# The first deformable tile of each group placed 24 plan units behind its places

## The reference, cut to what matters

```
x = x + L0(gn(x))   # focal modulation, three depthwise convolutions
x = x + L1(gn(x))   # fp8-quantised gated MLP per pixel
x = x + L2(gn(x))   # 7x7 circular convolutions, gates, scan over 8 steps
x = x + L3(gn(x))   # deformable 3x3 convolution
# L3: offsets = conv3x3(x) -> per pixel and tap a place (py, px)
#     val = sum of the 4 corners' values * bilinear weights  (9 taps, 64 channels)
#     out = einsum(val, kernel) + bias
```

## Time and profile before

| | us |
|---|---|
| median of 3 runs (lowest to highest) | 5486.43 (5479.14 to 5493.68) |
| the profiled execution's own time | 5502.65 |
| its span, first to last instruction | 5500.9 |
| busy: PE, DVE, POOL, ACT | 3035.7, 3300.6, 2874.9, 1728.7 |

### The profile page before, as it was taken

The page is one execution under the profiler, slowest core; times in us unless marked ns, Lnnn a source line. Parts: engine busy times, 40 slices in busy tenths (PEclk is TensorE's granted clock), DMA queues, the critical chain, the costliest instruction groups (busy, mean ns, idle before and its releaser), DMA issues. The chain is left out here.

```text
span 5500.9 us, 92960 instructions
## 1 busy us (share of the span) xinstructions
PE 3035.7 (55%) x39574; PEld 2637.7 (48%) x39574; DVE 3300.6 (60%) x4063; ACT 1728.7 (31%) x3209; POOL 2874.9 (52%) x2614
## 2 busy tenths in 40 slices
PE   2973235559744466569744466579744463454333
PEld 2872135459633365459633365469633353443222
DVE  4347843575678755565688656574788655454333
ACT  1223424621234235421233235421234242232000
POOL 1000000475566765565566655674666666677776
PEclk9965555569667766659767666659766666655555
DMA  6841184569633585559633576559633564754333
GB/s 164 171 91 22 33 133 138 141 147 224 146 96 102 129 193 169 148 135 222 146 94 105 133 178 173 153 144 236 139 107 98 144 172 136 173 171 131 112 106 93
DMA packets 776703, 763.09 MB, mean 139 GB/s; under 512 B 575185, under 2 KB 652401, under 8 KB 771857
## 3 DMA queue, kind: packets, MB, share of 16 engines
q1 hardware_dynamic: 651873, 417.24, 34.2%
q0 software_dynamic: 124416, 339.90, 21.8%
HBM read 637.12 MB, written 136.73 MB: 141 GB/s over the span
## 5 line engine op out<-in xcount | busy, mean ns | idle before, releaser
L2124 POOL DMA_INDIRECT e_gb<-corner_table,e_idx x2592 | 2860.3, 1104 | 2606.5 <-DMA e_cws<-cw_all 1097.6
L2186 DVE TENSOR_TENSOR e_vw<-e_gb,e_pc 128x1024 f32<-128x1024 f32 x576 | 774.9, 1373 | 710.4 <-DMA e_gb<-corner_table,e_idx 681.0
L2152 PE MATMUL e_pv<-shifts,e_vw 128*128 128x128 f32 x2744 | 536.7, 364 | 480.7 <-DVE e_vw L2193 480.7
L2152 PEld LDWEIGHTS e_pv<-shifts,e_vw 128*128 128x128 f32 x2744 | 440.0, 190 | 513.5 <-DVE e_vw L2193 491.2
L488 PE MATMUL e_pw<-wk,e_vt 128*64 128x64 f32 (+1 forms) x2880 | 324.4, 285 | 351.6 <-DVE e_xr L2204 220.3
L488 PEld LDWEIGHTS e_pw<-wk,e_vt 128*64 128x64 f32 (+1 forms) x2880 | 279.2, 192 | 413.7 <-issue 246.5
L2162 ACT ACTIVATE e_vt<-e_pv 128x512 f32<-128x512 f32 x288 | 183.6, 638 | 731.2 <-PE e_pw L2152 730.4
L502 PE MATMUL b_p<-b_x,b_tt 100*100 100x96 f32 x4096 | 396.2, 258 | 25.7 <-DMA b_tt<-zl_copies 25.0
L502 PEld LDWEIGHTS b_p<-b_x,b_tt 100*100 100x100 f32 x4096 | 388.6, 176 | 29.1 <-DMA b_tt<-zl_copies 28.2
L1921 ACT ACTIVATE f_xall<-f_p 64x384 f32<-64x384 f32 (+2 forms) x320 | 301.7, 1056 | 130.7 <-PE f_p L1816 128.4
L2193 DVE TENSOR_TENSOR e_vw<-e_vw 128x1152 f32<-128x1152 f32 x233 | 331.6, 1423 | 8.0
(11 more groups left out here) (309 smaller groups left out, 7147.3 us busy)
## 6 DMA issues: line engine op xcount, KB each, us to landing
b_tt<-zl_copies SPq DMA_DIRECT2D x256, 234.0 KB, 9.7
b_tt<-zl_copies SPq DMA_DIRECT2D x128, 390.0 KB
e_gb<-corner_table,e_idx POOLq DMA_INDIRECT x2592
d_px<-x_halo SPq DMA_DIRECT2D x32, 1152.0 KB
corner_table<-f_xn SPq DMA_DIRECT2D x128, 288.0 KB
f_xall<-xpad SPq DMA_DIRECT2D x10, 2400.0 KB, 16.7
x_halo<-d_xo SPq DMA_DIRECT2D x128, 144.0 KB
d_wd<-wd_rows SPq DMA_DIRECT2D x8, 1890.0 KB, 30.8
```

Source lines behind the costliest of these rows:

```text
L2124: nc.gpsimd.indirect_dma_start(self.gb[k][:, 4 * q:4 * q + 4, :].rearrange("p a c -> p (a c)"), None, T.table[m], off)\
L2152: last = nc.tensor.matmul(dst, vw[:, a, 2 * q:2 * q + nq, :].rearrange("p k c -> p (k c)"), T.ident[:, :], start=(a == 0), stop=(a == n - ...
L2186: v.tensor_tensor(dst, self.gb[k][:, 4 * k0:4 * k1, :].rearrange("p (k a) c -> p k a c", a=4), bc(w, [128, k1 - k0, 4, C], 3), ALU.mult).t ...
```

## The change

In `plan()`, where all loaded tiles are placed and an image's places have just been written, the next tile's due time is set 24 units later. Everything else follows from it.

```diff
             if StageF.placed(P, k) is not None:
                 if tiles == J * loaded:
-                    due = clock
+                    due = clock + 24.0
                 ready += 1
```

## The result

The kernel after takes 5447.58 us in the median (5443.26 to 5449.61, four runs), the kernel before 5490.06 us beside it (5479.14 to 5499.29, four runs): a ratio of 0.9924 with a 95% interval of [0.9911, 0.9937], 42 us faster. The forecast was 85 us faster. The direction was right and the time lies inside the range, but only half of the gain came.

What follows compares the result with a forecast made beforehand. Stages were taken to set the pace before 4592 us, with VectorE stalled at group starts, and GpSimd's gathers after. Terms -60 - 20 - 5 + 0 = -85 us took the 5486.43 median to 5401 us; 8-in-10 range 5371 to 5460.

Steps and rivals of the forecast that it cites:

- Part 1: Start of the first three groups: moving early tiles behind later steps ends VectorE's stall for gathers, 60.0 us less.
- Part 2: Rest of stage F, behind k11 to k17: VectorE's waits for gathers go, 20 us less, bounds 0 to 52.2.
- Part 3: Last group: GpSimd's wait for D k4's image shortens, 5 us less; bounds -19 and +23.
- Part 4: Phase: every other tile shifts against the stage steps, taken as 0 us, bounds -4 and +34.
- waiting pairs: Nine more stage steps with two tiles behind them, each waiting 3.81 us: the +34 us bound.
- Gathers beside VectorE's work: Start of groups: gathers may slow while VectorE writes, 2.1 us lost per group, making the sum 6 us smaller.
- Only the stall goes, and the phase gives some of it back: Rival, 0.17: groups' starting stall goes, -60 us, but nine more tile pairs wait, +34, giving 5460 us.
- The lead is absorbed: Rival, 0.08: something else paces stage F and the next stage starts no sooner, 5486 us, no change.
- The last group starts late: Rival, 0.09: GpSimd idles at the last group's head, +23 and +12 us, giving 5521 us.

Runs made afterwards that it cites:

- e6_48_rest: e5_48 with tiles 0 and 1 of the first three groups back behind k8 and k9, as in the kernel before: 5451.6 us, ratio 0.9928.
- e1_two_only: Kernel before with only tiles 0 and 1 of the first three groups moved, from behind k8 and k9 to behind k10: 5488.15 us, ratio 0.9988.
- f4_48_kept: Kernel before with tiles due 48 units later in the first three groups, nothing caught up, and 24 in the last: 5416.68 us, ratio 0.9862.
- e4_last_only: Kernel before with only the last group's tiles due 24 units later: 5486.44 us, ratio 0.9987.
- e5_48: Kernel before with tiles due 48 units later in the first three groups, caught up over each group's last tiles, 24 in the last: 5395.32 us, ratio 0.9825.
- e8_back_in_time: The change with its 24 units caught up over the last sixteen tiles of each of the first three groups: 5460.62 us, ratio 0.994.
- e3_both: Kernel before with the first three groups' tiles due 24 units later, caught up by the 16th tile, last group unchanged: 5455.81 us, ratio 0.9929.
- f3_last_48: Kernel before with only the last group's tiles due 48 units later: 5523.48 us, ratio 1.0056.

## Why the prediction was half right

**Part 1, 60 us forecast.** The size is right. Counted from ScalarE's instruction of the round before to the one that follows the norm (line 1985), the round of the first tiles took 66.9, 72.5 and 74.2 us in the kernel before and 51.0, 51.4 and 50.7 us in the one after: 15.9, 21.1 and 23.6 us, together 60.6 (forecast 18.0, 18.3, 23.7). That was luck as far as the reason goes: the reckoning took the times at which tiles end, and these are set by the gathers. The reason given with it, that an idle engine in the middle of a stage costs its full length, was wrong here, where GpSimd was the bound; e6_48_rest shows it right where GpSimd has to wait in turn. e1_two_only removes that wait and its first F stays at 117.1 us. Its norm started here, 4.5 us ahead of before's, with tile 2 weighed in front of it:

```profile
1062.96 0.28 DVE L445 TENSOR_REDUCE gn_ms<-f_p 96x64 f32<-96x128 f32 x1
```

The other 12 us of the 16 come from tile 2's leaving the round, 9 x 1.32 = 11.9 us of gathers.

**Part 2, 20 us forecast, 0 measured. This is the first step that failed**: "The waits go, but what is late next is ScalarE." They don't go (50.5 us for 52.2), and F as a whole gained 60.2 us (20.9, 26.2 and 13.1), no more than Part 1 alone. Behind the first round that is 5.0 and 5.1 us gained in the first two groups and 10.5 lost again in the third. Behind k8, GpSimd is the bound. Gathers issued from the first one to the last places, in the kernel before 81, 82 and 82, in the one after:

```profile
L2124 POOL DMA_INDIRECT e_gb<-corner_table,e_idx x63: 942/949/1972, 1023.2 to 1106.5; - x63
```

and 64 and 72 in the second and third group. That is 18, 18 and 10 fewer, or 23.8, 23.8 and 13.2 us at 1.32 each, 61 in all: the whole gain, and near each group's. It is one effect, and the prediction booked it twice: the tile that leaves the first round (in Part 1) is the tile fewer "up to the same step" (in Part 2). The prediction had the clue in its own sentence, that the five further tiles came "about as close as GpSimd supplies them". Twelve us times the tiles listed was the sum to make; instead the waits of the consumer were added up.

**Part 3, 5 us forecast, 6 to 8 measured.** 7.8 us between the two kernels; over the table the last column is 891.8 to 897.6 us in the four lists with the last group as before (mean 894.9) and 886.9 to 893.9 in the eight that shift it by 24 (mean 889.2, f4_48_kept left out), 5.7 us. Tile 216 was not late, and the load comes earlier as forecast: 12.3 us after D k0's norm (4589.41 - 4577.1) instead of 20.1 (4680.52 - 4660.4), 7.8 us sooner. The gap in front of D k4 shrank by more than that, from 19.12 to 4.09 us. What the prediction did not have is the 13.15 us ahead of tile 222, where gathers land late beside stage D's reads; they use up most of it. In all GpSimd idles 10.9 + 13.15 = 24 us there, where it was 32.3. The first gather to the end was to be 886 us or so; it is 882 (4546.7 to 5427.8, and 0.95 for the last).

**Part 4, 0 forecast, 15 to 28 lost. This is the second step that failed**, a term put at nothing, and with Part 2 it is where the other half went. The lead at the end of F, 60.2 us over three groups, is neither the 45.0 us that arrive at the last group, nor the 32.0 (by line 2052, 4570.02 - 4538.02) against e4_last_only, whose rest was shorter. The bounds (-4 to +34) held it, the price of waiting pairs was its only source and I took the end that was next to nothing. That the shift as such is the cause is excluded by e5_48 and f4_48_kept: with twice the shift their rest is 3206.4 and 3188.9 us. That it is the position ahead of the next k8 finds no support in e8_back_in_time, nor in e3_both. It goes with the tiles taken out of F, but not in proportion: the four lists that take out none have a rest of 3196.6 to 3210.4 us, the five that take out five tiles have 3216.8 to 3240.5, and yet those with nine have 3188.9 to 3213.7. What is left is how the tiles fall on the steps of stages A to D, one by one, and that is not settled: with 13 us between two executions of one list it can't be read tile by tile. TensorE's clock is a rival that no run tests: the rest of the three groups ran at a mean granted clock of 0.69, 0.69 and 0.69 of full speed after, and 0.71, 0.70 and 0.70 before.

**Gathers beside VectorE's work.** Among the 18 gathers of tiles 0 and 1 of the first group, which now run beside k10's work, the longest took this:

```profile
1038.40 1.33 POOL L2124 DMA_INDIRECT e_gb<-corner_table,e_idx  x1 [0.30 <-issue]
```

Some 0.4 us above the usual 0.95, where 2.1 us had been reckoned as a possible loss, and in the kernel before the longest of the same 18 took 1.34. The 18 gathers took 17.6 us together in both kernels. k10's last three VectorE instructions (1023.60 to 1029.90 us) cost nothing that can be told here: the five gathers issued from 1024.64 to 1029.65 us took 0.94 or 0.95 us each, and the first of all, at 1023.23, 1.11 us as in the kernel before. Beside the last group's `d_xo` (3.35 us from 4573.79 on) a gather again takes 3.09 us (at 4574.89). What lengthens it there is not shown.

**The rivals.** "Only the stall goes, and the phase gives some of it back" gave 5460 us at 0.17 and came nearest in effect: 60 us less, some of it given back. Its mechanism, pairs of tiles that wait 3.81 us each, was not what any run isolated. "The lead is absorbed" is out, 42 us arrived. "The last group starts late" did not happen but exists: f3_last_48 shows it with an idle time of 32.98 us (the rival had 23 and 12), and f4_48_kept has it by another way (11.12 us ahead of tile 217).

## What to carry to other kernels

Where a consumer waits for a producer that never pauses, as GpSimd in stage F, the waits aren't worth their length: count what the producer must deliver up to the end of the stage and multiply by its interval. Taking a wait away then only moves it, unless fewer items are asked for in that stage, and both together gain more than either (8, 21 and 40 us here). This holds as long as the stage's own steps are not the bound. Look for the optimum by the number of items: 48 units, three tiles out of F in each group, gained 101 us, 72 units 59 us and 96 units lost 9, because other stages have to take the tiles.

## What was not expected of the hardware

Executions of one kernel can differ by more than the change of a part. The kernel before, e4_last_only and f3_last_48 carry the same work in the same order up to tile 215, and yet the stretch between the second group's last and the third group's first places took 1107.2, 1094.2 and 1103.8 us; all other stretches agree within 1.5 us in the first two, and within 3.6 with the third. Nine of the 13 us lie in stage A at its head, which ends after 122.6, 113.8 and 114.2 us, and TensorE's granted clock goes with it. In the first 115 us it was 0.56 of full speed before, and TensorE was busy for 78.8 us with 958 matmuls; in e4_last_only it was 0.63, and 74.0 us for 1082; in f3_last_48 0.67, and 72.2 us for 1082. What set the clock is not shown, and f3_last_48 loses its 10 us later. A difference of two traces below some 15 us says nothing here about the change; the medians over several runs do.

Gathers landed late while other transfers filled the DMA engines: in the last group after, tile 220's first four were issued from 4596.8 to 4601.5 us and their weighing began at 4636.53, with the DMA engines busy for 0.99 of that time. GpSimd's own instruction takes its usual 0.95 us meanwhile, so its row doesn't show it.

An indirect gather of 128 rows occupies GpSimd for 0.95 us with 0.30 us to the next, and with the slower ones among them their distance was 1.32 us over 81 gathers (before), 1.34 over 63 (after, (1106.5 - 1023.2) / 62) and 1.34 over 54 (e5_48): close enough to one figure for a stage's supply.
